# Query maxima of an attention unit sent from SBUF to SBUF instead of by way of DRAM, in a fused attention and MoE block on one core

## The reference

```python
# block 1: attention with 16 heads of 8 columns, and an additive bias by distance
logits = jnp.einsum('bhld,bhmd->bhlm', q, k) * scale + bias[None]
attn = jax.nn.softmax(logits, axis=-1)
out = jnp.einsum('bhlm,bhmd->bhld', attn, v)
# block 2: attention again, without bias, with a projection, then a mixture of 8 experts
x = x + _msa(_layernorm(x, ln1_w, ln1_b), w_qkv, w_proj)
x = x + _moe_mlp(_layernorm(x, ln2_w, ln2_b), gate_w, gate_b, w1, w2)
```

## Time and profile before

| | |
|---|---|
| median of 3 runs | 975.05 us |
| lowest and highest | 971.11 and 975.51 us |
| profiled execution | 976.09 us |
| its span, first to last instruction | 974.3 us |
| PE, DVE, ACT, POOL busy | 86%, 73%, 64%, 25% |
| DMA queue of SP (q1), share of 16 engines | 24.9% |

### The profile page before, as it was taken

How to read it: one execution, slowest core, us unless ns; L and a number is a source line. 1 busy time by engine, 2 the same in 40 slices (tenths; PEclk the granted TensorE clock), 3 DMA queues, 4 the chain that set the end, 5 groups by cost and what they waited for, 6 DMA issues and landing times.

```text
span 974.3 us, 22607 instructions
## 1 busy us (share of the span) xinstructions
PE 833.8 (86%) x8987; PEld 317.3 (33%) x8987; DVE 709.6 (73%) x1133; ACT 626.3 (64%) x1227; POOL 243.9 (25%) x543
## 2 busy tenths in 40 slices
PE   4289999999989899999997889899889999646680
PEld 2023333333333333333321232222323222236670
DVE  5387866777768767777787859899777997155344
ACT  6037766777756667777776779899667999401121
POOL 5010044300004444200004616011040101005663
PEclk9569999999999999999998899999989999867896
DMA  3745453655554344653132233422212220101123
GB/s 100 202 141 168 158 154 121 196 172 161 172 169 143 123 144 121 193 181 123 52 97 67 84 84 111 119 64 76 67 42 66 70 67 24 36 22 31 46 41 94
DMA packets 69438, 104.82 MB, mean 108 GB/s; under 512 B 15814, under 2 KB 45958, under 8 KB 69334
## 3 DMA queue, kind: packets, MB, share of 16 engines
q1 hardware_dynamic: 63254, 68.90, 24.9%
q10 hardware_dynamic: 4608, 31.46, 9.2%
q0 software_dynamic: 1472, 3.02, 1.3%
HBM read 84.23 MB, written 19.01 MB: 106 GB/s over the span
## 4 chain that ended last, share of the span: by engine, by line
PE 58%; DVE 11%; POOL 9%; DMA 5%; SPq 5%; ACT 5%; issue 4%; another core or an unknown queue 1%; POOLq 0%; DVEq 0%; ACTq 0%
PE bank L1183 18%; PE bank L1208 14%; PE bank L1215 11%; PE bank L1162 7%; ACT prob_mem L820 4%; POOL norm L594 3%; DVE no_use L909 3%; DVE unit_max L912 3%; DVE stats L858 2%; PE bank L1374 2%; PE bank L1365 2%; POOL rstd L588 2%; DMA prob_mem<-unit_sums 2%; PE bank L1134 1%; POOL y_res L594 1%
## 5 line engine op out<-in xcount | busy, mean ns | idle before, releaser
L820 ACT ACTIVATE prob_mem<-bank 128x512 f32<-128x512 f32 x1024 | 557.2, 599 | 164.1 <-PE bank L1215 123.5
L909 DVE CUSTOM_DVE_ANT_0 no_use<-bank,w_moe 128x1024 bf16<-128x1024 f32 x256 | 311.6, 1223 | 109.8 <-PE bank L1162 109.7
L1162 PE MATMUL bank<-k_rows,q_rows 56*128 56x512 bf16 x1024 | 320.3, 398 | 29.3 <-DMA k_rows<-k_parts 18.0
L1208 PE MATMUL bank<-q_rows,k_rows 59*128 59x512 bf16 x1024 | 329.4, 391 | 7.3 <-DMA q_rows<-maxima_rows 3.5
L1183 PE MATMUL bank<-prob_mem,v_ring 128*32 128x256 f32 x4096 | 324.3, 391 | 7.2 <-issue 6.1
L912 DVE TENSOR_REDUCE unit_max<-bank 128x1 f32<-128x1024 f32 x256 | 297.3, 1218 | 39.5 <-PE bank L1162 37.6
L630 POOL CAST max_parts<-unit_max 128x8 bf16<-128x8 f32 x64 | 12.2, 191 | 589.5 <-DVE unit_max L909 327.5
L1215 PE MATMUL bank<-skew_mem,flip 96*32 96x512 bf16 x2048 | 159.6, 389 | 0.0
L1208 PEld LDWEIGHTS bank<-q_rows,k_rows 59*128 59x128 bf16 x1024 | 80.6, 94 | 239.2 <-issue 125.2
L1183 PEld LDWEIGHTS bank<-prob_mem,v_ring 128*32 128x32 f32 x4096 | 102.9, 110 | 168.2 <-ACT prob_mem L820 64.6
L1162 PEld LDWEIGHTS bank<-k_rows,q_rows 56*128 56x128 bf16 x1024 | 76.0, 94 | 41.9 <-issue 19.3
(11 more groups left out here) (166 smaller groups left out, 506.6 us busy)
## 6 DMA issues: line engine op xcount, KB each, us to landing
w_moe<-bias_rows ACTq DMA_DIRECT2D x32, 960.0 KB, 5.6
q_rows<-q_parts SPq DMA_DIRECT2D x256, 48.0 KB
k_rows<-k_parts SPq DMA_DIRECT2D x128, 96.0 KB
skew_mem<-bias_parts SPq DMA_DIRECT2D x32, 378.0 KB, 4.4
unit_sums<-o_ring SPq DMA_DIRECT2D x64, 128.0 KB, 2.1
w_moe<-in_L_ffn_w_dram SPq DMA_DIRECT2D x16, 256.0 KB, 3.1
q_parts<-prob_mem SPq DMA_DIRECT2D x8, 384.0 KB, 3.1
k_parts<-prob_mem SPq DMA_DIRECT2D x24, 128.0 KB, 2.6
```

Of the source, the lines that this page charges most:

```text
L820: nc.scalar.activation(prob[:, kb, half * N:(half + 1) * N], b_bank(entry(n, kb, half)), ACT.Exp).then_inc(exp_done, 1)
L909: nc.vector.tensor_tensor_reduce(out=no_use[:, qb % 2, :], in0=scores, in1=bias, scale=1.0, scalar=LEAST, op0=ALU.add, op1=ALU.max, accum_ ...
L1162: return nc.tensor.matmul(place[:, f, :], q_rows[rows, m % SLOTS, qb * P:(qb + 1) * P], k_rows[rows, m % SLOTS, f * N:(f + 1) * N], start= ...
L1208: return nc.tensor.matmul(b_bank(entry(n, kb, f)), k_rows[rows, n % SLOTS, kb * P:(kb + 1) * P], q_rows[rows, n % SLOTS, f * N:(f + 1) * N ...
```

## The change

`maxima_of` no longer uses DRAM. For each half f of the queries and each part t, one transfer takes four rows of 128 of `max_rows` in SBUF to 512 columns of one partition of `q_rows` in SBUF: six transfers in place of one store and two loads, with no wait between them. The DRAM tensor and the semaphore of the store go away. The semaphore of the loads now counts 96 instead of 32 for a unit, at PE's wait too, and ACT's wait before it writes a slot of `max_rows` again is now for the transfers of the unit two before, and no longer for its store.

```diff
@@ maxima_of(n), on SP
                 slot = n % 2
                 sp.wait_ge(max_copied, n + 1)
-                sp.dma_start(maxima_dram[slot], max_rows[:, slot, :]).then_inc(mrow_stored, 16)
-                sp.wait_ge(mrow_stored, 16 * (n + 1))
-                maxima = maxima_dram[slot].rearrange("(p q) c -> p (q c)", p=3)
                 for f in range(2):
-                    sp.dma_start(q_rows[f * HP + KR:f * HP + KR + 3, n % SLOTS, f * N:(f + 1) * N],
-                                 maxima[:, f * N:(f + 1) * N]).then_inc(mrow_loaded[slot], 16)
+                    for t in range(3):
+                        sp.dma_start(q_rows[f * HP + KR + t:f * HP + KR + t + 1, n % SLOTS, f * N:(f + 1) * N],
+                                     max_rows[t * QB + f * TG:t * QB + (f + 1) * TG, slot, :]).then_inc(mrow_loaded[slot], 16)
@@ maxima_out(n, src), on ACT
                 if n >= 2:
-                    act.wait_ge(mrow_stored, 16 * (n - 1))
+                    act.wait_ge(mrow_loaded[n % 2], 96 * (n // 2))
                 nc.scalar.copy(max_rows[:, n % 2, :], src).then_inc(max_copied, 1)
@@ the unit loop, on PE
-                pe.wait_ge(mrow_loaded[n % 2], 32 * (n // 2 + 1))
+                pe.wait_ge(mrow_loaded[n % 2], 96 * (n // 2 + 1))
```

More of the change, by code:

```diff
@@ L67, in sandwich_kernel @@
     o_dram = nc.dram_tensor("unit_sums", (U, P, W), fp32, kind="Internal").ap()
-    maxima_dram = nc.dram_tensor("maxima_rows", (2, 3 * QB, P), bf16, kind="Internal").ap()
     bias_dram = nc.dram_tensor("bias_rows", (H, 2 * L), fp32, kind="Internal").ap()
@@ L250, in sandwich_kernel @@
         max_copied = sem("max_copied")
-        mrow_stored = sem("mrow_stored")
         mrow_loaded = [sem(f"mrow_loaded{s}") for s in range(2)]
```

## The result

The changed kernel takes 983.7 us in the median of 4 runs (979.8 to 985.91), the kernel before 975.28 us beside it: a ratio of 1.0092, 95% interval 1.0047 to 1.0137. A second set of six runs gave 983.15 us and 1.0084 (1.0059 to 1.0108). It is slower, by 8 us, and outside the range of 966.5 to 981.5 us.

The account below looks back on a forecast made before the run. Quiet units were taken to lose nothing, with gains only where SP runs behind or its transfers queue. 0.1 + 1.36 + 0.3 + 1.3 + 0.0 = 3.1 us off the median of 975.05 us gave 972.0 us, range 966.5 to 981.5 us.

Parts of the forecast that it names:

- The price of an issue: SP's queue, six new transfers: 0.31 us each with the gap, taken from line 458; range 0.27 to 0.64 us.
- 290 us: PE's wait for a batch's sums: SP issues them 1.79 us earlier, of which 1.3 us is taken as gain.
- The dearer issue: Rival, chance 0.20: each issue on SP's queue costs 0.64 us like line 476; 6.1 us slower, 981.2 us.
- the sums of 502 and 685 us: PE's waits for the sums of two later batches: SP leaves the maxima hardly earlier, gain 0.0 us at both.
- 613 and 622 us: PE's waits for the maxima in two neighbouring places: gain 1.36 us at the first, a further 0.3 us at the second.
- 411 and 424 us: Places where PE starts slightly late on the maxima: the six transfers land in time, gain 0.1 us.
- ACT's wait: ACT's new wait for the transfers of the unit two before: it never stands and costs nothing.
- the first unit: Maxima copied at 50 us while DVE is at those of the second unit; PE starts after DVE, no gain.
- 613 us: PE's stop for the maxima, which SP reaches late at 608.58: gain 1.36 us, 1.9 us of the stall stay.
- Hidden anyway: Rival, chance 0.17: bytes in the queue bind 290 us, weights ahead bind 613 us; only 0.6 us won, 974.4 us.
- faster: Rival, chance 0.15: landing 1.0 us, the full 1.79 us at 290 us, SP earlier near 600 us; 5.2 us won, 969.9 us.
- Each waits out the one before: Rival, chance 0.01: six transfers in series take 7.6 us in each unit, about 140 us slower, 1115 us.
- Only above 0.63 us: Issue price above which SP's 1.9 us free in a quiet unit are gone and some 30 units each pay.

Follow-up runs that it names:

- the filled ones: Products that nobody reads put inside PE's waits for the first three sums: changed kernel 977.41 us (1.0016), kernel before 968.45 us (0.9937).
- zeros from DRAM: The changed kernel with its six transfers reading rows of 512 zeros from DRAM instead of the maxima: 967.58 us, ratio 0.9895 to the kernel before.
- eight issues: The changed kernel with eight transfers of 3 rows x 128 in place of the six: 1030.09 us, ratio 1.0574 to the kernel before.
- three extra ones: The kernel before with three more transfers of four rows to one behind the maxima in every unit, to a tile nobody reads: 999.92 us, ratio 1.0292.
- the earlier sums: The loads of the sums moved ahead of the ten row loads: kernel before 960.69 us (0.9826), changed kernel 965.88 us (0.9894).

## Why the prediction was wrong, point by point

*The price of an issue* is the step that failed. The sum took 0.31 us, "the issue of the nearest one, line 458, which writes the same partitions". Nearest was the wrong word: it shares the destination and not the pair of memories. Measured are 0.57 us, 0.61 to 0.63 with the gap. The trace of before did hold a transfer within SBUF, the filling of the minus-one rows at 5 us, issued at 713 and 970 ns for its two:

```profile
L416 SPq DMA_DIRECT2D k_rows<-minus x2: 713/842/970, 5.0 to 6.0; - x2
```

I saw it and left it out, because of its size. It was the only row of the right kind, and it would have made the dear price the likelier one. With the price as measured SP has no time to give back: instead of leaving the maxima 1.8 us earlier at 290 us it leaves them 0.2 us later, and at the other places, where the sum had gains of 1.8 us, PE's stops grow by 6.4 us.

*The dearer issue* was therefore the case that happened, at a chance of 0.20. It had the places right: 3.9 us at the sums of 502 and 685 us (PE stood 3.6 us longer there: 8.25 against 4.60 us), some at 290 us (0.2 us longer, 3.55 against 3.33 us), 2.0 us around 613 and 622 us, where the stops are 2.2 us longer. Its price was right by an unlike row: line 476 is dear between DRAM and SBUF, and the new form is dear because both its ends are in SBUF. Its time, 981.2 us, was 2 to 2.5 us short of the medians. The range was said to take in both ends of the price and the spread of the runs, but its top, 981.5 us, is only 0.3 us above this rival's time, so no spread was added at that end.

*The clock* has no term in the prediction. It costs several us at PE's stops in both kernels, as the filled ones show. In the one pair of profiles the longer stops were followed by more of the lower level, but the filled pair stays 9.0 us apart. So it is not shown that the missing term made the forecast wrong. What makes up the last 2 us or so of the loss, beyond the stops, stays open.

*411 and 424 us, ACT's wait, the first unit*: as predicted, nothing. The unit table stays within 0.7 us up to unit 34, and ACT never waited for the transfers.

*613 us* was to gain 1.36 us. The six issues from 612.54 us ended at 616.34, and PE went on at 617.41 us, 1.6 us after the start of the sixth issue. With 5 x 0.64 = 3.2 instead of 1.55 us ahead of the sixth, the step's own working gives a start 0.3 us later than before, and that is the change of the stop, 3.14 to 3.48 us. The stops of 1.04 and 1.14 us beside it had no term, or less.

*Hidden anyway* and *faster* assumed the cheap price and did not arise; with zeros from DRAM the 1.3 us at 290 us were won, against the first of them. *Each waits out the one before* is refuted by the same place: PE went on 1.6 us after the sixth was issued, where the rival has 1.26 us for each of six. That six issues without a wait, at a cheap price, are faster than before, the run with zeros from DRAM shows, and with a larger gain than the sum.

*Only above 0.63 us* for quiet units: there the price is at 0.63 and the spare time at 0.46 us with no quiet unit lost, though it is a close thing: from 638 to 675 us PE's weight load stands 0.41 us for the maxima in every unit. So the threshold was about right, and the experiments beyond it (eight issues, three extra ones) show what lies there.

What stays open: 1 to 5 us of what was won with zeros from DRAM, and 6 to 10 us of what was won by the earlier sums. Each profile is a single execution, and spells at half clock fall in different places from one to the next.

## What to carry to other kernels

The time for which a queue issues is a resource like an engine's, and its price goes by the form of the transfer, both memories included; look for a row of the same pair before taking a cheap neighbour. Removing a wait from a queue does not help the work behind it if the queue is then busy for longer than it waited. A stop of PE can cost more than its length by the clock behind it, here some 1.5 to 2 us at each stop for the sums. Set loads that PE waits for ahead of loads that have units of slack, which here won 1.7%, and compare a loop unit by unit before explaining a total.

## What the runs showed of the hardware

- Issuing a small transfer on SP's queue: 1.10 to 1.26 us for four with DRAM on one side, 2.45 to 2.83 us for four within SBUF, whatever the patterns, and 2.42 us for four that each read four separate rows of DRAM into one row of SBUF. Four rows of SBUF to one contiguous run in DRAM are cheap, 1.25 us for four.
- Landing behind the end of the issue, on an empty queue: 1.05 to 1.20 us to SBUF, from either memory, 0.91 us to DRAM.
- In the two profiles of the changed kernel, stops of PE of 3.0 to 5.0 us for the sums were followed by a granted clock of 0.50 for 3.4 to 6.9 us; with PE kept busy for 2.98 us of such a stop the clock stayed at 1.00. The length of the stop does not tell what follows. After 1.99 us (502 us, before) and 3.14 us (613 us, before) the clock stayed at 1.00; after 2.61 us (685 us, before) and 4.47 us (617 us, filled) the lower level held for 3.4 us; and in the run with zeros from DRAM a stop of only 1.51 us was followed by 10 us of it, the longest spell behind any of them:

```profile
502.85 0.39 PE L1227 MATMUL bank<-ident,prob_mem 16*128 16x16 f32 x4 [1.51 <-DMA prob_mem<-unit_sums]
```

```profile
505.00:510.00 5.00, 5.00 (x30) 1.47 (x30) 3.73 (x4) 2.55 (x5) 0.00 (x0) 0.50 0.39 110
510.00:515.00 5.00, 5.00 (x30) 1.20 (x30) 3.56 (x5) 2.17 (x4) 0.93 (x5) 0.50 0.24 72
```
